# Graph network, four layers: the third layer's attention split by query halves, with projection, norm and first feed-forward product of the first half placed beside the second half's tail

## What is computed

```python
q = (x @ Wq + bq).reshape(N, H, HEAD)          # k and v likewise
scores = jnp.einsum('nhd,mhd->nhm', q, k) / np.sqrt(HEAD)
adj = jnp.zeros((N, N), jnp.float32).at[edge_index[0], edge_index[1]].set(1.0)
scores = jnp.where(adj[:, None, :] == 0, -1000000000.0, scores)
attn = jax.nn.softmax(scores, axis=1)          # over the heads
attn_out = jnp.einsum('nhm,mhd->nhd', attn, v).reshape(N, D_OUT)
attn_out = attn_out @ Wo + bo
h1 = _layer_norm(x + attn_out, g1, be1)
ff = jax.nn.relu(h1 @ W1 + b1) @ W2 + b2       # W1: 512x1024, W2: 1024x512
return _layer_norm(h1 + ff, g2, be2)
```

## Time and profile before

| | |
|---|---|
| median of 3 launches | 566.43 us (566.41 to 567.49) |
| the profiled execution | 569.44 us, of which its span 567.5 us |
| mean granted TensorE clock in it | 0.949 |
| busy: PE, DVE, ACT, POOL | 84%, 57%, 28%, 25% of the span |
| the third layer's attention loop | from 352.3 us to 428.97 us |
| behind it, up to the first product of `FF` | up to 487.33 us |

### The profile page before, as it was taken

One profiled execution on the slowest core, in us unless ns is written; L12 is line 12 of the kernel. 1 busy time (PEld: TensorE's weight loads), 2 busy tenths in 40 slices (PEclk: granted clock), 3 DMA queues, 4 the chain that ended last, 5 costly groups with the idle time before them and its releaser, 6 DMA issues.

```text
span 567.5 us, 6449 instructions
## 1 busy us (share of the span) xinstructions
PE 478.6 (84%) x2089; PEld 269.4 (47%) x2089; DVE 325.7 (57%) x574; ACT 159.6 (28%) x326; POOL 144.0 (25%) x154
## 2 busy tenths in 40 slices
PE   5789968877765999998999999567839599998996
PEld 2423336545454999543444444445524244444442
DVE  6987767778769974478416100699970800147214
ACT  1221136545436574221111012233322211102010
POOL 9100005433359100031202500366543300002000
PEclk9999989999998699998999999899988779999998
DMA  8700000000005002565110010000000000000001
GB/s 282 270 1 0 1 0 3 1 1 2 1 20 205 1 2 80 217 241 204 72 59 0 13 62 0 1 0 1 1 0 0 0 1 0 0 1 0 1 0 74
DMA packets 13598, 25.76 MB, mean 45 GB/s; under 512 B 896, under 2 KB 1280, under 8 KB 13568
## 3 DMA queue, kind: packets, MB, share of 16 engines
q1 hardware_dynamic: 13568, 25.38, 12.6%
HBM read 24.33 MB, written 1.05 MB: 45 GB/s over the span
## 4 chain that ended last, share of the span: by engine, by line
PE 59%; DVE 29%; issue 5%; ACT 2%; DVEq 2%; POOL 2%; ACTq 0%; POOLq 0%
PE ring L1086 35%; PE banks L1244 6%; PE ring L1092 4%; DVE G L1043 3%; DVE G L1039 3%; PE ring L1163 3%; PE ring L1172 3%; DVE G L1054 3%; DVE W_SD L807 3%; DVE W_SD L814 3%; PE ring L1341 2%; DVE G L872 2%; DVE st L921 1%; PE ring L1328 1%; DVE X L721 1%
## 5 line engine op out<-in xcount | busy, mean ns | idle before, releaser
L434 POOL TENSOR_TENSOR A_SD<-A_SD,HH 128x128 f32 x64 | 34.2, 535 | 116.5 <-ACT HH L569 102.6
L950 DVE TENSOR_TENSOR HH<-ring,RB 128x512 f32<-128x512 f32 x16 | 11.0, 686 | 76.1 <-PE ring L1086 59.7
L458 POOL TENSOR_TENSOR RB<-X,vec 128x512 f32<-128x512 f32 x16 | 22.6, 1418 | 118.2 <-DVE X L946 116.8
L1200 PE MATMUL banks<-RB,WB 128*128 128x128 f32 x256 | 44.8, 302 | 0.0
L1039 DVE TENSOR_REDUCE G<-ring 128x256 f32<-128x2048 f32 x8 | 18.3, 2292 | 35.8 <-PE ring L1328 35.6
L519 ACT ACTIVATE WA<-ring 128x512 f32<-128x512 f32 x44 | 25.3, 592 | 47.5 <-PE ring L1092 47.3
L1200 PEld LDWEIGHTS banks<-RB,WB 128*128 128x128 f32 x256 | 36.7, 204 | 0.0
L781 DVE TENSOR_REDUCE HH<-banks 128x6 f32<-128x768 f32 x32 | 30.5, 957 | 10.5 <-PE banks L1156 10.5
L533 ACT ACTIVATE sd<-mv,eps 128x1 f32<-128x1 f32 x32 | 9.4, 294 | 93.7 <-DVE mv L926 93.7
L491 POOL TENSOR_TENSOR G<-G 128x1024 f32<-128x1024 f32 x8 | 19.0, 2378 | 62.7 <-ACT G L639 44.5
L1244 PE MATMUL banks<-VB,WA 128*128 128x64 f32 x256 | 32.7, 292 | 0.0
(11 more groups left out here) (175 smaller groups left out, 914.0 us busy)
## 6 DMA issues: line engine op xcount, KB each, us to landing
WA<-in_wqkv SPq DMA_DIRECT2D x2, 1024.0 KB, 8.2
WC<-in_w SPq DMA_DIRECT2D x2, 1024.0 KB, 8.2
WB<-in_wo SPq DMA_DIRECT2D x2, 1024.0 KB, 6.6
WA<-in_w SPq DMA_DIRECT2D x2, 1024.0 KB, 8.9
G<-in_w SPq DMA_DIRECT2D x1, 2048.0 KB, 16.0
WA<-in_xT SPq DMA_DIRECT2D x4, 256.0 KB, 4.0
WA<-in_wqkv SPq DMA_DIRECT2D x4, 256.0 KB, 4.2
vec<-in_g SPq DMA_DIRECT2D x4, 256.0 KB, 7.8
```

What stands on the lines that cost most here:

```text
L434: pool.tensor_tensor(win, win, cnt_g[:, q, :, :], ALU.add).then_inc(group_added, 1)
L458: pool.tensor_tensor(out_, x_, vec[:, slot[vector], :], ALU.add).then_inc(resid_ready, 1)
L1200: last = nc.tensor.matmul(weights, src_wide[:, slot_, q, :, j], weight_hot[:, slot_, q, :, j], start=False, stop=(j == 1), skip_group_chec ...
```

## The change

The units run through the first half of the queries for all four key blocks (u = 0 to 3) and then through the second half (u = 4 to 7). `out_of` puts the first half's output into `bank[0..1]` and the second's into `bank[2..3]`, so the first half is complete after unit 3. On ACT `take_out(0)` copies it ahead of `exp2(7)`. On PE the projection of the blocks 0 and 1 (`side_product`) stands among the last `heads_out`, in `bank[0]` and `bank[1]`; the blocks 2 and 3 follow when the second half is done. DVE's `affine_norms` runs first for blocks 0 and 1 (`take_side`), then for 2 and 3. `FT` becomes 16 products of 256 queries (`hidden`): 8 for the first half, between which the banks 0 and 1 alternate, then the transposes of blocks 2 and 3, then 8 for the second half. DVE instead of POOL makes the head sums of the last unit. `FT` moves to `WA[:, 1:3]`, and `w3` to `G[:, 0:4096]`, loaded once all heads are in.

```diff
-    for b in range(NB):
+    for b in range(NB // 2, NB):
         add("WO2", (b,), "D")
-    for b in range(NB):
+    for b in range(NB // 2, NB):
         add("HT2", (b,), "A")
...
             load("w12a", WC[:, :, :], blocks(a["w12"][:, 0:D]))
+            sp.wait_ge(out_full, 2 * NB)
+            load("w3a", w3[:, 0, :, :], blocks(a["w3"][0:D, :]))
+            load("w3b", w3[:, 1, :, :], blocks(a["w3"][D:2 * D, :]))
...
-            for u in range(NU):
+            for u in range(NU - 1):
                 pool.wait_ge(soft_exp, u + 1)
...
+            def take_out(half):
+                n = slice(half * UN, (half + 1) * UN)
+                for i in range(2):
+                    act.wait_ge(out_full, NB + 2 * half + i + 1)
+                    act.activation(XT[:, 2 * i:2 * i + 2, n], bank[2 * half + i].rearrange("p (j n) -> p j n", n=UN),
+                                   ACT.Copy).then_inc(out_taken, 1)
...
             for u in range(NU):
+                if u == NU - 1:
+                    take_out(0)
                 exp2(u)
                 if u:
                     invert(u - 1)
             invert(NU - 1)
...
+            take_out(1)
+            for _ in range(3):
+                std()
+            for b in range(NB // 2):
+                act.wait_ge(side_full, 2 + b + 1)
+                act.activation(XT[:, :, b * P:(b + 1) * P], bank[b].rearrange("p (k n) -> p k n", k=NB),
+                               ACT.Copy).then_inc(side_evacuated, 1)
             std()
...
+            for f in range(2 * NB):
+                act.wait_ge(side_full, 4 + f + 1)
+                rectified(f, 0, bank[f % 2][:, 0:UN])
+            for b in range(NB // 2, NB):
                 turned(("HT2", b), XT, b)
...
+            dve.wait_ge(soft_exp, NU)
+            e, t = sT[:, (NU - 1) % 4, :, :], sum_tree[:, (NU - 1) % 2, :, :]
+            link(dve.tensor_tensor(t, e[:, 0:4, :], e[:, 4:8, :], ALU.add))
+            link(dve.tensor_tensor(t[:, 0:2, :], t[:, 0:2, :], t[:, 2:4, :], ALU.add))
+            dve.wait_ge(soft_sum, NU - 1)
+            dve.tensor_tensor(t[:, 0, :], t[:, 0, :], t[:, 1, :], ALU.add).then_inc(soft_sum, 1)
             weigh(NU - 2)
             weigh(NU - 1)
...
-            affine_norms("WO2", 4 * NB, "g12", vec[:, slot["be12"], :])
+            affine_norms("WO2", 4 * NB, "g12", vec[:, slot["be12"], :], 0, NB // 2, True)
+            affine_norms("WO2", 4 * NB, "g12", vec[:, slot["be12"], :], NB // 2, NB)
...
+            def side_product(b):
+
+                if b == 0:
+                    pe.wait_ge(out_taken, NB + 2)
+                for k in range(NB):
+                    last = nc.tensor.matmul(bank[b], cols(XT, k, b), WB[:, k, :], start=(k == 0), stop=(k == NB - 1))
+                last.then_inc(side_full, 1)
+
+            def hidden(f, half, t):
+                w1 = WC if f < NB else W_SD
+                for k in range(NB):
+                    last = nc.tensor.matmul(t, cols(w1, k, f % NB), XT[:, k, half * UN:(half + 1) * UN], start=(k == 0),
+                                            stop=(k == NB - 1))
+                last.then_inc(ring_full if half else side_full, 1)
...
+            for u in range(NU):
+                scores(u)
+                others_out(u)
+                if u == NU - 1:
+                    pe.wait_ge(loads["wo2"], 16)
+                    side_product(0)
                 if u >= 3:
                     heads_out(u - 3)
...
+            side_product(1)
+            for u in range(NU - 3, NU):
+                heads_out(u)
+            for b in range(NB // 2, NB):
+                if b == NB // 2:
+                    pe.wait_ge(out_taken, 2 * NB)
+                product(("WO2", b), lambda k: cols(XT, k, b), lambda k: WB[:, k, :])
+            for b in range(NB // 2):
+                pe.wait_ge(side_taken, b + 1)
+                pe.wait_ge(h_ready, NB + b + 1)
+                for k in range(NB):
+                    last = nc.tensor.transpose(bank[b][:, k * P:(k + 1) * P], cols(HH, b, k), ident[:, :])
+                last.then_inc(side_full, 1)
...
+            for f in range(2 * NB):
+                pe.wait_ge(side_evacuated, f + 1)
+                hidden(f, 0, bank[f % 2][:, 0:UN])
+            for b in range(NB // 2, NB):
                 pe.wait_ge(h_ready, NB + b + 1)
                 turn(("HT2", b), lambda k: cols(HH, b, k))
             wait_emptied(pe, ("HT2", NB - 1))
...
             for f in range(2 * NB):
...
+                hidden(f, 1, claim(("FT", f))[:, 0:UN])
```

More of the change, by code:

```diff
@@ L955, in take_scaled, with take_side, affine_norms @@
                                          op1=ALU.add).then_inc(dve_emptied, 1)
-            def affine_norms(name, resids, gain, shift):
+            def take_side(b):
+                dve.wait_ge(side_full, b + 1)
+                dve.tensor_tensor(HH[:, b, :], bank[b], RB[:, b, :], ALU.add).then_inc(side_taken, 1)
+            def affine_norms(name, resids, gain, shift, first=0, end=NB, side=False):
                 taken = [None] * NB
-                for b in range(NB + 1):
-                    if b < NB:
+                for b in range(first, end + 1):
+                    if b < end:
                         dve.wait_ge(resid_ready, resids + b + 1)
-                        take((name, b), HH[:, b, :], RB[:, b, :])
-                    if b:
-                        r = inverse_std(taken[b - 1])
-                    if b < NB:
-                        wait_emptied(dve, (name, b))
+                        if side:
+                            take_side(b)
+                        else:
+                            take((name, b), HH[:, b, :], RB[:, b, :])
+                    if b > first:
+                        r = inverse_std(taken[b - 1])
+                    if b < end:
+                        if side:
+                            dve.wait_ge(side_taken, b + 1)
+                        else:
+                            wait_emptied(dve, (name, b))
                         spread = spread_of(HH[:, b, :])
-                    if b:
+                    if b > first:
                         c = centered(HH[:, b - 1, :], gain, r[1])
-                    if b < NB:
+                    if b < end:
                         taken[b] = moments(spread)
-                    if b:
+                    if b > first:
                         scaled(HH[:, b - 1, :], HH[:, b - 1, :], shift, r, c).then_inc(h_ready, 1)
@@ L1300, in others_out @@
                 for j in range(H // 2):
[L1301 to L1302 removed]
+                    nc.tensor.matmul(out_of(j, half), cols(VB, m, j), NADJ[:, m, half * UN:(half + 1) * UN],
+                                     start=(m == 0 and j % 2 == 0), stop=False, skip_group_check=True)
             def heads_out(u):
[L1305 removed]
@@ L1313, in heads_out, with scores @@
                         last.then_inc(out_full, 1)
-                if u < NU - 1:
+                if m < NB - 1:
                     last.then_inc(head_done, 1)
+            def scores(u):
+                m, n = u % NB, slice(u // NB * UN, (u // NB + 1) * UN)
+                for p in range(0, H // 2, 2):
+                    pair = [claim(("ST", u, p)), claim(("ST", u, p + 1))]
+                    for i in range(2):
+                        for j, t in enumerate(pair):
+                            h = UNIT_HEADS[2 * (p + j) + i]
+                            r = slice((h % 2) * HD, (h % 2 + 1) * HD)
+                            last = nc.tensor.matmul(t[:, i * UN:(i + 1) * UN], KB[r, h // 2, m * P:(m + 1) * P],
+                                                    QB[r, h // 2, n], start=True, stop=True)
+                            if i == 1:
+                                last.then_inc(ring_full, 1)
@@ L1334, in _ @@
                 if u >= 3:
                     heads_out(u - 3)
-            pe.wait_ge(loads["wo2"], 16)
-            for k in range(NB):
-                pe.wait_ge(out_taken, NB + k + 1)
-                for b in range(NB):
-                    t = claim(("WO2", b)) if k == 0 else bank_of(("WO2", b))
-                    last = nc.tensor.matmul(t[:, :], cols(XT, k, b), WB[:, k, :], start=(k == 0), stop=(k == NB - 1))
-                    if k == NB - 1:
-                        last.then_inc(ring_full, 1)
```

71 lines of the change are left out of this document (29 added, 42 removed).

## The result

| | before | the change |
|---|---|---|
| median of the launches beside each other (4 each) | 566.89 us | 546.99 us (545.98 to 548.92) |
| ratio, 95% interval | | 0.9664 (0.9617 to 0.971) |
| profiled execution: own time, span | 569.44, 567.5 us | 546.77, 544.7 us |
| start of the attention loop | 352.34 us | 349.60 us |
| scores of the last unit | 404.60 us | 402.62 us |

A forecast was written before the change was run, and what follows sets the result against it. DVE was taken to pace the attention loop up to 412 us, then one serial chain to the second product. Its start moves from 487.33 to 468.95 us, 18.4 less: 566.43 - 18.4 = 548.0 us, range 543 to 554.

The forecast's parts named there:

- the clock ahead of the first product: PE at the start of `FT`: slow records after a long pause, bounds 0 and 3.4 us, 2.5 taken.
- Side products in the idle time, at no cost: PE among the last heads: two side products of 3.45 us each from 408.5 us, using 6.9 us of idle time.
- Head sum on DVE: Last unit: `weigh(7)` ends at 422.7 instead of 425.23 us, last heads at 424.7, 4.3 us earlier, if the clock holds.
- the side products delay the heads: Rival, last heads: `take_out(0)` falls behind `exp2(7)`, last heads end some 6 us later, 554 us; 3%.
- the clock falls before the projection: Rival, last heads and projection: three 0.7 us pauses count like one long one, losing 1.7 and 3.4 us, 553 us; 14%.
- Projection over 11.7 us earlier: PE behind the last heads: blocks 2 and 3 take 6.9 us, over at 432.3 instead of 444.0 us.
- The new wait: ACT ahead of `FT`: copies wait for the third square root, at 435.45 us including 2.7 us of POOL contention.
- nothing collides: Rival, norms of blocks 0 and 1: no DVE and POOL collision, and the clock stays, 543 us; 10%.
- Start of the first product: PE after the first copies: `FT` starts at 436.7 instead of 455.77 us.
- 128 records of 256 columns in 27.5 us: PE in `FT`: 128 records of 256 columns at 0.215 us each replace 64 of 512.
- half the columns don't take half the time: Rival, `FT`: at the full width's 0.433 us a record it takes 55.4 us, giving 576 us; 3%.
- Units in another order, and `w3` later: nothing: Attention loop and loads: same instructions at about 7.5 us a unit, `w3` lands before about 495 us; no cost.

The follow-up runs named there:

- e3: The changed kernel with the projection of blocks 0 and 1 made behind the last heads instead of among them; 553.19 us, ratio to before 0.9725.
- e1: The changed kernel with the head sum of the last unit back on POOL instead of DVE; 554.61 us, ratio to before 0.9746.
- e4: The changed kernel with POOL's eight residuals made only once all four blocks are normed; 545.63 us, ratio to before 0.9595.
- e10: The changed kernel with POOL's residuals behind all norms, ACT's copies ahead of the third square root, and hidden products of 128 columns, not 256; 547.69 us.
- e11: The changed kernel once more, with no edit, in a later group; 548.84 us, ratio to before 0.97.
- e7: The changed kernel with ACT's copies of the transposes of blocks 0 and 1 behind the fourth square root; 552.49 us, ratio to before 0.9785.
- e8: The kernel before with only the head sum of the last unit moved from POOL to DVE; 563.31 us, ratio to before 0.9963.

## Why the prediction was right, point by point

The order of the new chain and its waits came as forecast, and so did nearly all its terms; the one mis-sized term is the clock ahead of the first product. That the median came within 1 us owes something to luck: the clock term was 2.5 us too large for the trace of the change, and the same kernel gave 548.84 us in a later group, in which the kernel before had 565.09 and not 566.43.

Times are from the scores of the last unit (404.60 before, 402.62 after).

- **Side products in the idle time, at no cost.** Forecast start 3.9 us in, measured 3.76. Right; ACT's two copies were over 0.2 us before, and its `exp2(7)` still waited for DVE, so the rival "the side products delay the heads" did not come: the heads of unit 6 waited 0.55 us for DVE. e3 prices the cover at 5.0 us.
- **Head sum on DVE: 2.5 us, and a clock that holds.** Last heads over at 20.1 forecast, 20.0 measured. Right, and e1 shows both halves of it. The rival "the clock falls before the projection" did not come: after pauses of 0.55, 0.84 and 0.70 us heads and projection ran at the full rate.
- **Projection over 11.7 us earlier.** 27.7 forecast, 27.7 measured. Right.
- **The new wait: the third square root ahead of the copies.** I had it over at 30.85 us, and it was at 30.38. The collision with POOL was sized at three of four operations, 2.7 us; it was three of four, 2.5, and e4 takes it away with POOL alone, for 1.9 us of the stage. The rival "nothing collides" is out. Right, but three of four was a pick between none and all, with nothing that said which would be spared.
- **Start of the first product** at 32.1; measured 31.61.
- **128 records of 256 columns in 27.5 us, half of the full width each.** 27.97 measured, 0.218 each; right to 2%. The rival that half the columns don't take half the time has no support, and at a quarter of the width it is 3% more (e10).
- **Transposes and copy between the halves**: 1.75, measured 1.77.
- **The clock ahead of the first product, 2.5 us.** This is the term that was mis-sized. In the profiled execution it was 0, in e11 1.7. I had called the pause "of the long kind", with only transposes in 4.4 us; PE had only transposes in 3.9 us, and the last pause was 2.33 us, after which the clock went either way. I had also read too little of the trace of before: "after pauses of 2.95 to 4.39 us the next work ran slow" leaves out the 2.89 and 3.02 us at 367.67 and 374.61 us, behind which it didn't. At 4.39 us it does cost 3.0 (e7).
- **Sum.** 18.4 us forecast; 20.8 in the stage of the first trace, 19.1 in e11 (82.73 - 63.66), 19.9 by the medians. The 2.4 us between 18.4 and 20.8 are the clock term (2.5) and three small ones: 0.5 us less to the product's start, 0.5 more in its records, 0.1 more at its end. In the later group it is 16.3 us by the medians (565.09 - 548.84), so the forecast lies between the two groups; the 20.8 us rest on one trace of before, which may have had more slow stretches than most (e8).
- **Units in another order, and `w3` later: nothing.** From the start of the loop to the scores of the last unit it is 52.26 us before and 53.02 in the change, 52.39 in e11; the 0.8 us are a slow stretch (3.55 instead of 2.00 us for unit 2's scores). Behind the second product's start nothing changed (80.17 and 80.12).
- **Nothing upstream.** The loop started 2.7 us earlier in the trace of the change, but it lies between 349.6 and 355.2 us in all thirteen traces, the change's own second one at 349.61 and the variants' up to 355.15. In the trace of before, one such slow stretch stands in the second layer (eight records 5.40 us, after a pause of 2.48; the same row of the change takes 3.70, and of e11 5.36). That is 1.7 of the 2.7 us; 1.05 came before it. Nothing here puts it down to the change.

## What to carry to other kernels

When an attention stage ends in a serial tail of projection, norm and product, splitting by output rows lets PE work on one half beside the element-wise tail of the other; ask for each half what an idle engine could already do, and order the units so that a half is complete early. In fp32, halving the columns from 512 to 256 cost about 1% here (27.97 against 27.73 us for the same columns), and 128 another 3%, so it is cheap as long as it buys cover. Price a pause twice: by its length and by the slow records behind it; what waits on other engines (a sum on POOL, one square root too early in ACT's queue) cost through the clock was about as much as their length (2.3 us beside 2.6 in e1, 3.0 beside 2.06 in e7).

## What the runs showed of the hardware that I had not expected

After a pause of 2.33 us with eight short transposes before it, the same product ran once at the full rate (7.14 us) and once partly at half (8.83 us), in two traces of one kernel. After 0.55 to 1.70 us behind work at the full rate it always stayed there in the last units, after 3.74 and 4.39 us never: 3.29 to 3.68 instead of 1.95 us for heads, 10.15 instead of 7.14 for the product, and 9.64 instead of 7.13 for the projection right behind such heads. Between them, at 2.3 to 3.0 us, both came. This is a likely part of what makes launches of one kernel differ by several us (not shown, as one launch of each has a trace). An edit worth under 2 us can be read from a stage of the trace, once the slow records in it are counted apart (1.7 us in e11), but not from the medians of six launches.

Beside POOL, a 128x512 centering or scaling of DVE took 1.46 to 1.65 instead of 0.72 to 0.75 us when it started while POOL's addition was running. When it had started 0.08 to 0.16 us ahead of POOL's, as at 451.51 before and at 428.73 and 435.42 in the change, it kept its length. That held in the norms behind this layer's attention in all nine traces where POOL ran beside them; four centerings at whose start a POOL addition was in its last 0.2 us kept their length too.
